# Row-sum reciprocals taken two tiles at a time, with each tile's probabilities made two steps behind its scores

## The chip, the cores and the metric

The kernel runs on one NeuronCore of a Trainium2 chip. The metric is the device time of one launch in microseconds (us); the core has a matrix engine (PE), a vector engine (DVE), a scalar engine (ACT), GpSimd (POOL), and a sync engine (SP) that issues the DMAs.

## The reference, cut to what matters

One decoder layer on x of shape 4 x 512 x 512 in float32: attention with low-rank query and key/value projections, 16 heads and rotary parts, then a quantised cross block, then a mixture of experts. The change touches the softmax of the attention:

```
scores = jnp.einsum('blhd,bmhd->bhlm', q, k) * scale
mask = jnp.tril(jnp.ones((L, L), bool))
scores = jnp.where(mask[None, None], scores, jnp.array(-1e+30, scores.dtype))
attn = jax.nn.softmax(scores, axis=-1)
out = jnp.einsum('bhlm,bmhd->blhd', attn, v)
```

With 4 batches and 16 heads there are 64 heads of 512 x 512 causal scores.

## The kernel before

Two heads make a pair, so `walk` runs over 32 pairs i = 0 to 31 (written out, no loop on the chip). A pair has eight steps g = 0 to 7: the four row tiles k = g & 3 of its first head, then those of its second. Tile k has (k + 1) x 128 columns, because of the causal mask. G = 8 i + g counts tiles over all pairs. Every engine has its own `pair` function with its instructions in a fixed order, and semaphores join the engines.

One tile goes through this chain:

- PE, `scores` (L1733 to L1738): six products into one of three PSUM banks.
- DVE, `row_max` (L1414): the negated row maximum. POOL, `bias` (L1018): times the scale.
- ACT, `exps` (L1160): the exponential into PF, with its row sum into one column of SUM.
- DVE, `row_scale` (L1421, L1423): reciprocal of the sum, times 4096.
- DVE, `probs_hi` (L1431) and `probs_lo` (L1438): the normalised tile as two fp16 parts in PH, high and rest.
- SP, `turn_probs` (L971): a DMA that transposes both parts into PT.
- PE, `values` (L1750): once for each head, after all its four transposes: the product with the values. `values(i, 0)` stands at step 7 of pair i, `values(i-1, 1)` at step 4.

Between these, each step carries other work. On DVE these are the low halves of two PSUM read-outs (`out_lo` L1444 at steps 0 and 5, `qn_lo_` L1449 at steps 2 and 6), the rotary part of the next pair (`rotate`, L1457, L1461 and L1462, at step 4; its copies L1466 and L1470 at step 7), and `add_y` (L1477). The rotary chain goes from `rotate` on DVE to `rope_sum` on POOL (L1022), `rope_hi` on ACT (L1176, L1177) and `rope_t_hi` on PE (L1690, step 6). On ACT, `out_hi` (L1165) of step 5 stands behind `rope_hi` in program order, and DVE's `out_lo` of step 5 waits for it. After `values(i, 0)` PE goes on with the scores of the next pair. From pair 4 on PE also runs `project` (L1765).

Even pairs below 24 also prepare a token tile of the next batch (`prep`): DVE's `prep_lo` (L1355, step 1) releases PE's `prep_t` (L1638), and later PE runs `prep_mm` (L1649). Pairs 24 to 31 have no such work.

At the end, SP issues `first_weights` (L369, four loads, 3 MB together) behind the transpose of tile 3 of pair 31 and ahead of those of tiles 4 to 7, on the same queue.

`turn_probs` and the release of `exps` wait on `s_lo`, the count of finished `probs_lo`; `probs_hi` waits until the tile before it in the same part of PH has been transposed.

Of the kernel before, what the change touches and what calls it, by code (L numbers as in the profile page):

```python
# [26 lines left out]
NPAIR = B * H // 2  # L27
# [3 lines left out]
PSCALE = 4096.0  # L31
# [4 lines left out]
def decoder_layer(nc, x, fside, ctxw, w_qa, q_norm_w, w_qb, w_kva, kv_norm_w, w_kvb, w_o,  # L36
                  router_w, w1, w2, w3, rope_tab, out):
    fp32, fp16, bf16, u32 = mybir.dt.float32, mybir.dt.float16, mybir.dt.bfloat16, mybir.dt.uint32
    ALU, ACT, AX = mybir.AluOpType, mybir.ActivationFunctionType, mybir.AxisListType
# [4 lines left out]
    def sem(name):  # L44
        return es.enter_context(nc.semaphore(name))
# [7 lines left out]
    with es:  # L53
# [26 lines left out]
        def take(cols, dt=fp32):  # L80
# [46 lines left out]
        NEGM, NB, SUM, RC, R4 = (small[:, 20 + 4 * k:24 + 4 * k] for k in range(5))  # L127
# [43 lines left out]
        s_mm, s_max, s_bias, s_exp, s_rc, s_hi, s_lo = (  # L171
            sem(n) for n in ("s_mm", "s_max", "s_bias", "s_exp", "s_rc", "s_hi", "s_lo"))
        pt_in = [sem(f"pt_in{k}") for k in range(TB)]
        s_r4 = sem("s_r4")
# [70 lines left out]
        def pf(k):  # L245
            return PF[:, k * (k + 1) // 2 * P:(k + 1) * (k + 2) // 2 * P]
# [4 lines left out]
        def ph_part(k, hl):  # L251

            return ph(k).rearrange("p (t l c) -> p t l c", l=2, c=P)[:, :, hl, :]
# [19 lines left out]
        def started(q):  # L273

            return not (isinstance(q, int) and q < 0)
# [960 lines left out]
        def _(dve):  # L1236
# [173 lines left out]
            def row_max(G, g):  # L1410

                n = ((g & 3) + 1) * P
                dve.wait_ge(s_mm, G + 1)
                dve.tensor_reduce(NEGM[:, (g & 3):(g & 3) + 1], banks[S_BANKS[g % 3]][:, 0:n], AX.X, ALU.max,  # L1414
                                  negate=True).then_inc(s_max, 1)

            def row_scale(G, g):

                k = g & 3
                dve.wait_ge(s_exp, G + 1)  # L1420
                dve.reciprocal(RC[:, k:k + 1], SUM[:, k:k + 1]).then_inc(s_rc, 1)  # L1421
                dve.wait_ge(s_rc, G + 1)
                dve.tensor_scalar(R4[:, k:k + 1], RC[:, k:k + 1], PSCALE, None, ALU.mult).then_inc(s_r4, 1)  # L1423

            def probs_hi(i, g):

                k, G = g & 3, 8 * i + g
                dve.wait_ge(s_r4, G + 1)
                if not (isinstance(i, int) and i == 0 and g < 4):
                    dve.wait_ge(pt_in[k], 16 * (2 * i + (g >> 2)))  # L1430
                dve.tensor_scalar(ph_part(k, 0), pf(k).rearrange("p (t c) -> p t c", c=P), R4[:, k:k + 1], None,  # L1431
                                  ALU.mult).then_inc(s_hi, 1)

            def probs_lo(G, g):

                k = g & 3
                dve.wait_ge(s_hi, G + 1)
                dve.scalar_tensor_tensor(out=ph_part(k, 1), in0=pf(k).rearrange("p (t c) -> p t c", c=P),  # L1438
                                         scalar=R4[:, k:k + 1], in1=ph_part(k, 0), op0=ALU.mult,
                                         op1=ALU.subtract).then_inc(s_lo, 1)  # L1440

            def out_lo(Hd, gpar, slot):
                dve.wait_ge(o_hi, Hd + 1)
                dve.tensor_tensor(ot(gpar, 1, slot, 0, L), banks[O_BANK][:, :], ot(gpar, 0, slot, 0, L),  # L1444
                                  ALU.subtract).then_inc(o_lo, 1)

            def qn_lo_(Hd, h):
                dve.wait_ge(qn_hi, Hd + 1)
                dve.tensor_tensor(qn(h, 1, 0, L), banks[Q_BANK][:, :], qn(h, 0, 0, L), ALU.subtract).then_inc(qn_lo, 1)  # L1449
# [14 lines left out]
            def rope_out_hi(i, par):  # L1464
                dve.wait_ge(r_th, i + 1)
                dve.tensor_copy(QR[:, par * 1536:par * 1536 + 1024], bank16[R_BANK]).then_inc(r_teh, 1)  # L1466

            def rope_out_lo(i, par):
                dve.wait_ge(r_tl, i + 1)
                dve.tensor_copy(QR[:, par * 1536 + 1024:(par + 1) * 1536],  # L1470
                                bank16[Q_BANK][:, 0:L]).then_inc(r_tel, 1)
# [8 lines left out]
            def pair(i, j, first=False, last=False, prep=None):  # L1480
                G = 8 * i
                for g in range(8):
                    if g == 7 and not last:
                        rope_out_hi(i + 1, 1 - j)
                    row_max(G + g, g)
                    if g > 0:
                        row_scale(G + g - 1, g - 1)
                    elif not first:
                        row_scale(G - 1, 7)

                    if g == 2:
                        qn_lo_(2 * i + 1, 1)
                    if g == 4 and not last:
                        rotate(i + 1)
                    if g == 5 and not first:
                        Hd = 2 * i - 1
                        out_lo(Hd, (Hd >> 3) & 1, Hd & 7)
                    if g == 6 and not last:
                        qn_lo_(2 * i + 2, 0)
                    if g == 7 and not last:  # L1500
                        rope_out_lo(i + 1, 1 - j)
                    if prep is not None and j == 0:
                        if g == 0:
                            prep_ln(prep[0])
                        if g == 1:
                            prep_lo(prep[0])
                    if g > 0:
                        probs_hi(i, g - 1)
                        probs_lo(G + g - 1, g - 1)
                    elif not first:  # L1510
                        probs_hi(i - 1, 7)
                        probs_lo(G - 1, 7)
                    if prep is not None and j == 0:
                        if g == 0:
                            prep_xn(prep[0])
                        if g == 3:
                            prep_var(prep[0])
                            prep_rope(prep[0], prep[2])
                            prep_srq(prep[0])
                            prep_rope_sum(prep[0])  # L1520
                        if g == 5:
                            prep_split(prep[0])
                    if g == 0 and not first:
                        Hd = 2 * i - 2
                        out_lo(Hd, (Hd >> 3) & 1, Hd & 7)
                    if prep is not None and j == 1 and g == 1:
                        prep_out(*prep)
                    if (j, g) in ADD and started(i - ADD[j, g]):
                        add_y(i - ADD[j, g])
# [39 lines left out]
            rope_out_lo(0, 0)  # L1569
            qn_lo_(0, 0)  # L1570
            walk(pair)
            row_scale(8 * NPAIR - 1, 7)
            probs_hi(NPAIR - 1, 7)
            probs_lo(8 * NPAIR - 1, 7)
            out_lo(2 * NPAIR - 2, 1, GH - 2)
            out_lo(2 * NPAIR - 1, 1, GH - 1)
            for q in range(NPAIR - 5, NPAIR):
# [290 lines left out]
```

## Time and profile before

| | |
|---|---|
| median of three runs | 1356.03 us (1355.33 to 1356.2) |
| profiled execution, device time | 1356.68 us |
| its span, first to last instruction | 1354.9 us |
| DVE busy | 1088.9 us (80%) |
| PE busy | 1039.2 us (77%) |
| ACT busy | 539.4 us (40%) |
| POOL busy | 239.7 us (18%) |
| pairs 0 to 31 | about 172 to 943 us of the span |

Times in a timeline count from the start of the span. A row of a timeline gives start, duration, engine, line, operation, output and input, and in brackets how long the engine had been idle and who ended that. DVE's durations overlap a little: the next instruction usually starts some 0.07 us before the last one's end is recorded. So what an instruction costs is read from start to start.

### The profile page before, as it was taken

The page shows a single profiled execution, that of the slowest core. Times are in us where ns is not written, and L with a number is a line of the kernel's source. Part 1 is how long each engine was busy: PE and PEld are TensorE (multiplying, and loading weights), DVE is VectorE, ACT ScalarE, POOL GpSimd, SP SyncE. Part 2 cuts the span into 40 slices and gives each one's busy share as a digit, 9 for nine tenths or more (in the row PEclk, how much of TensorE's full clock was granted, in tenths as well). Part 3 has the DMA queues.
Part 4 walks back from the last instruction along what each step waited for, and adds up shares of the span by engine and source line. Part 5 has one row for each costly group of instructions (what it writes and reads, how often), then busy time and mean ns, then how long its engine had stood idle before and what let it go on. Part 6 is the DMA issues. An engine that isn't in the chain of part 4 may idle for free.

```text
span 1354.9 us, 22533 instructions
## 1 busy us (share of the span) xinstructions
PE 1039.2 (77%) x7438; PEld 632.5 (47%) x7460; DVE 1088.9 (80%) x2984; ACT 539.4 (40%) x1225; POOL 239.7 (18%) x475
## 2 busy tenths in 40 slices
PE   1635687799999999998999999997743552547998
PEld 0423354455555555555555565564332231324554
DVE  5679587988888988988988988887179878876886
ACT  1539444434434434344444444443024321533443
POOL 1000012112112112112112121211022313131111
PEclk9659889999999999999999999999875776767999
DMA  9100022332332342322442333455361000000001
GB/s 360 55 1 0 1 53 49 73 58 57 58 56 54 65 116 53 66 55 46 70 119 47 66 61 61 94 92 147 79 218 39 24 31 0 0 0 8 39 31 47
DMA packets 199388, 86.30 MB, mean 64 GB/s; under 512 B 173560, under 2 KB 184824, under 8 KB 198784
## 3 DMA queue, kind: packets, MB, share of 16 engines
q1 hardware_dynamic: 199296, 85.12, 26.9%
q8 instruction: 52, 0.85, 0.3%
q14 instruction: 40, 0.33, 0.1%
HBM read 35.80 MB, written 7.34 MB: 32 GB/s over the span
## 4 chain that ended last, share of the span: by engine, by line
PE 40%; DVE 25%; issue 23%; ACT 5%; POOL 5%; DMA 1%; ACTq 0%; SPq 0%; DVEq 0%; POOLq 0%
PE bank L1765 10%; PE bank L1715 5%; DVE arena L1438 4%; PE bank L1649 4%; PE bank L1750 4%; DVE arena L1414 3%; PE bank L1681 2%; DVE arena L1431 2%; POOL arena L418 2%; PE bank L1733 2%; PE bank L1737 2%; PE bank L1735 2%; PE bank L1734 2%; PE bank L1736 2%; DVE scal L1532 1%
## 5 line engine op out<-in xcount | busy, mean ns | idle before, releaser
L1160 ACT ACTIVATE arena<-bank,arena,scal 128x128 f32<-128x128 f32 (+3 forms) x256 | 157.9, 617 | 356.6 <-POOL arena L1018 356.6
L1765 PE MATMUL bank<-arena 128*128 128x512 f16 x768 | 187.8, 391 | 7.1 <-DVE arena L1477 4.3
L1438 DVE SCALAR_TENSOR_TENSOR arena<-arena 128x128 f16<-128x128 f32 (+3 forms) x256 | 169.3, 661 | 9.1
L1414 DVE TENSOR_REDUCE arena<-bank 128x1 f32<-128x128 f32 (+3 forms) x256 | 124.2, 485 | 60.4 <-PE bank L1738 60.3
L1018 POOL TENSOR_TENSOR arena<-arena,scal 128x1 f32<-128x1 f32 x256 | 49.0, 191 | 551.2 <-DVE arena L1414 551.2
L1715 PE MATMUL bank<-arena 128*128 128x512 f16 x576 | 136.4, 382 | 0.5 <-DVE arena L1470 0.5
L1750 PE MATMUL bank<-arena 128*128 128x512 f16 (+3 forms) x768 | 116.8, 302 | 10.8 <-DMA arena<-arena 10.8
L1765 PEld LDWEIGHTS bank<-arena 128*128 128x128 f16 x768 | 73.6, 100 | 90.4 <-issue 16.5
L1431 DVE TENSOR_SCALAR arena<-arena 128x128 f16<-128x128 f32 (+3 forms) x256 | 109.9, 429 | 3.0 <-issue 0.3
L1750 PEld LDWEIGHTS bank<-arena 128*128 128x128 f16 x768 | 70.3, 99 | 50.4 <-issue 13.1
L1733 PE MATMUL bank<-arena 128*128 128x128 f16 (+3 forms) x256 | 77.3, 302 | 4.7 <-issue 3.3
L1715 PEld LDWEIGHTS bank<-arena 128*128 128x128 f16 x576 | 54.0, 99 | 55.5 <-issue 1.9
L1737 PE MATMUL bank<-arena 128*128 128x128 f16 (+3 forms) x256 | 77.3, 302 | 0.0
L1735 PE MATMUL bank<-arena 128*128 128x128 f16 (+3 forms) x256 | 77.3, 302 | 0.0
L1736 PE MATMUL bank<-arena 128*128 128x128 f16 (+3 forms) x256 | 77.3, 302 | 0.0
L1734 PE MATMUL bank<-arena 128*128 128x128 f16 (+3 forms) x256 | 77.3, 302 | 0.0
L816 PE MATMUL bank<-identb,arena 128*128 128x128 bf16 x192 | 24.7, 289 | 66.6 <-DVE arena L659 61.4
L1649 PE MATMUL bank<-arena 128*128 128x384 f16 (+1 forms) x384 | 59.0, 317 | 18.8 <-DVE arena L1259 15.3
L1681 PE MATMUL bank<-arena 128*128 128x128 f16 x1152 | 71.0, 221 | 1.5 <-DVE arena L1309 1.5
L1681 PEld LDWEIGHTS bank<-arena 128*128 128x128 f16 x1152 | 67.0, 99 | 5.8 <-DVE arena L1309 1.9
L1444 DVE TENSOR_TENSOR arena<-bank,arena 128x512 f16<-128x512 f32 x64 | 44.0, 688 | 28.8 <-ACT arena L1165 28.8
L1022 POOL TENSOR_TENSOR arena<-arena 128x512 f32<-128x512 f32 x32 | 45.8, 1430 | 109.7 <-DVE arena L1462 109.7
(213 smaller groups left out, 2119.7 us busy)
## 6 DMA issues: line engine op xcount, KB each, us to landing
arena<-in_L_attn_w_qb SPq DMA_DIRECT2D x1, 4608.0 KB, 23.5
arena<-in_x SPq DMA_DIRECT2D x4, 1024.0 KB, 5.9
arena<-in_L_attn_w_o SPq DMA_DIRECT2D x1, 4096.0 KB, 33.9
arena<-arena SPq DMA_TRANSPOSE x256, 2.8
arena<-in_fside_BxS2xS SPq DMA_DIRECT2D x4, 1024.0 KB, 5.7
arena<-in_L_ffn_w SPq DMA_DIRECT2D x8, 512.0 KB, 8.3
out<-arena SPq DMA_DIRECT2D x16, 256.0 KB, 2.0
arena<-in_x SPq DMA_DIRECT2D x12, 256.0 KB, 3.0
```

The costliest lines, as they stand in the source:

```text
L1160: act.activation(pf(k), banks[S_BANKS[g % 3]][:, 0:n], ACT.Exp, bias=NB[:, k:k + 1], scale=sc_exp, accum_out=SUM[:, k:k + 1]).then_inc(s_e ...
L1414: dve.tensor_reduce(NEGM[:, (g & 3):(g & 3) + 1], banks[S_BANKS[g % 3]][:, 0:n], AX.X, ALU.max, negate=True).then_inc(s_max, 1)
L1431: dve.tensor_scalar(ph_part(k, 0), pf(k).rearrange("p (t c) -> p t c", c=P), R4[:, k:k + 1], None, ALU.mult).then_inc(s_hi, 1)
L1438: dve.scalar_tensor_tensor(out=ph_part(k, 1), in0=pf(k).rearrange("p (t c) -> p t c", c=P), scalar=R4[:, k:k + 1], in1=ph_part(k, 0), op0= ...
L1649: last = pe.matmul(banks[bank][:, 0:wid], XNT[:, (a * DC + c) * P:(a * DC + c + 1) * P], WA[:, w:w + wid], start=(k == 0), stop=(k == 3 * ...
L1681: last = pe.matmul(banks[R_BANK][:, t * P:(t + 1) * P], ct(bp, a, c, t * P, P), wr(b, c, i & 7), start=(k == 0), stop=(k == 3 * QC - 1))
L1715: last = pe.matmul(banks[Q_BANK][:, :], wq(a, c, (i & 7) * 2 + h), ct(bp, b, c, 0, L), start=(k == 0), stop=(k == 3 * QC - 1))
L1733: pe.matmul(bank[:, 0:n], qn(h, 0, q, P), ct(bp, 0, QC, 0, n), start=True, stop=False)
L1734: pe.matmul(bank[:, 0:n], qn(h, 0, q, P), ct(bp, 1, QC, 0, n), start=False, stop=False)
L1735: pe.matmul(bank[:, 0:n], qn(h, 1, q, P), ct(bp, 0, QC, 0, n), start=False, stop=False)
L1750: last = pe.matmul(banks[O_BANK][:, kt * P:L], cn(bp, a, kt), pt(h, b, kt, kt * P, L - kt * P), start=(kt == 0 and n == 0), stop=(kt == TB ...
L1765: last = pe.matmul(banks[Y_BANK][:, :], ot(gp, a, k, (q & 3) * P, P), wo(b, gp * GH + k), start=(k == 0 and n == 0), stop=(k == GH - 1 and ...
```

## The change

`row_scale` becomes `row_scales`: on even steps only, one reciprocal and one multiplication of two adjacent columns, for the tiles of the two steps before. `probs_hi` and `probs_lo` of a tile move from one step behind its scores to two. After the last pair, two tiles instead of one are left to normalise.

```diff
-            def row_scale(G, g):
-                k = g & 3
-                dve.wait_ge(s_exp, G + 1)
-                dve.reciprocal(RC[:, k:k + 1], SUM[:, k:k + 1]).then_inc(s_rc, 1)
-                dve.wait_ge(s_rc, G + 1)
-                dve.tensor_scalar(R4[:, k:k + 1], RC[:, k:k + 1], PSCALE, None, ALU.mult).then_inc(s_r4, 1)
+            def row_scales(G):
+                k, n = G & 3, G // 2
+                dve.wait_ge(s_exp, G + 2)
+                dve.reciprocal(RC[:, k:k + 2], SUM[:, k:k + 2]).then_inc(s_rc, 1)
+                dve.wait_ge(s_rc, n + 1)
+                dve.tensor_scalar(R4[:, k:k + 2], RC[:, k:k + 2], PSCALE, None, ALU.mult).then_inc(s_r4, 1)
-            def probs_hi(i, g):
-                k, G = g & 3, 8 * i + g
-                dve.wait_ge(s_r4, G + 1)
-                if not (isinstance(i, int) and i == 0 and g < 4):
-                    dve.wait_ge(pt_in[k], 16 * (2 * i + (g >> 2)))
+            def probs_hi(G):
+                k = G & 3
+                dve.wait_ge(s_r4, G // 2 + 1)
+                if G >= 4:
+                    dve.wait_ge(pt_in[k], 16 * (G // 4))
@@ pair
                     row_max(G + g, g)
-                    if g > 0:
-                        row_scale(G + g - 1, g - 1)
-                    elif not first:
-                        row_scale(G - 1, 7)
+                    if g % 2 == 0 and G + g >= 2:
+                        row_scales(G + g - 2)
...
-                    if g > 0:
-                        probs_hi(i, g - 1)
-                        probs_lo(G + g - 1, g - 1)
-                    elif not first:
-                        probs_hi(i - 1, 7)
-                        probs_lo(G - 1, 7)
+                    if G + g >= 2:
+                        probs_hi(G + g - 2)
+                        probs_lo(G + g - 2, g - 2)
@@ after the walk
-            row_scale(8 * NPAIR - 1, 7)
-            probs_hi(NPAIR - 1, 7)
-            probs_lo(8 * NPAIR - 1, 7)
+            row_scales(8 * NPAIR - 2)
+            for g in (6, 7):
+                probs_hi(8 * NPAIR - 8 + g)
+                probs_lo(8 * NPAIR - 8 + g, g)
```

## Rows read from the trace of the kernel before

**Rows 1.** The page, part 2: busy tenths in 40 equal slices.

```profile
PE   1635687799999999998999999997743552547998
DVE  5679587988888988988988988887179878876886
```

**Rows 2.** Waits between 172 and 945 us: total us, times, longest.

```profile
DVE arena L1414 <- PE bank L1738: 59.7, 77, 2.4
...
PE bank L1690 <- ACT arena L1177: 32.4, 18, 3.9
PE bank L1638 <- DVE arena L1355: 13.1, 11, 2.8
```

**Rows 3.** DVE's groups of instructions: busy us, mean ns, idle before.

```profile
L1421 DVE RECIPROCAL arena<-arena 128x1 f32<-128x1 f32 x256 | 39.1, 153 | 0.0
...
L642 DVE RECIPROCAL arena<-arena 128x4 f32<-128x4 f32 x16 | 2.8, 178 | 0.6
```

**Rows 4.** Timeline of DVE in pair 17 (odd), and one `probs_lo` of 512 columns.

```profile
606.43 0.34 DVE L1431 TENSOR_SCALAR arena<-arena 128x256 f16<-128x256 f32 x1
...
606.81 0.48 DVE L1438 SCALAR_TENSOR_TENSOR arena<-arena 128x256 f16<-128x256 f32 x1
...
607.53 0.69 DVE L1414 TENSOR_REDUCE arena<-bank 128x1 f32<-128x512 f32 x1 [0.24 <-PE bank L1738]
608.13 0.15 DVE L1421 RECIPROCAL arena<-arena 128x1 f32<-128x1 f32 x1
...
608.51 0.61 DVE L1431 TENSOR_SCALAR arena<-arena 128x384 f16<-128x384 f32 x1
...
610.82 0.69 DVE L1457 TENSOR_TENSOR arena<-bank,arena 128x512 f32<-128x512 f32 x1
...
615.39 0.69 DVE L1444 TENSOR_TENSOR arena<-bank,arena 128x512 f16<-128x512 f32 x1 [0.56 <-ACT arena L1165]
...
624.48 0.75 DVE L1438 SCALAR_TENSOR_TENSOR arena<-arena 128x512 f16<-128x512 f32 x1
```

**Rows 5.** Timeline of PE in pair 17: last score product of tile 4, and `values(17, 0)`.

```profile
609.62 0.22 PE L1738 MATMUL bank<-maskb,identb 128*128 128x128 bf16 x1
...
619.76 1.79 PE L1750 MATMUL bank<-arena 128*128 128x512 f16 x12
```

**Rows 6.** SP's transpose of a 512-column tile of pair 17, issue and landing.

```profile
L971 SPq DMA_TRANSPOSE arena<-arena x1: 1232/1232/1232, 614.3 to 614.3; - x1
...
DMA to landing us min/median/max: 3.1/3.1/3.1
```

**Rows 7.** Timeline of DVE and of PE in pair 18 (even, with `prep`).

```profile
622.10 0.28 DVE L1414 TENSOR_REDUCE arena<-bank 128x1 f32<-128x128 f32 x1
...
639.12 0.69 DVE L1457 TENSOR_TENSOR arena<-bank,arena 128x512 f32<-128x512 f32 x1
...
643.23 0.62 PE L1690 MATMUL bank<-ident,arena 128*128 128x128 f16 x8 [2.25 <-ACT arena L1177]
...
650.12 0.22 PE L1733 MATMUL bank<-arena 128*128 128x128 f16 x1 [0.54 <-issue]
```

**Rows 8.** Timeline of PE in pair 16: `project` behind such a wait.

```profile
592.66 3.76 PE L1765 MATMUL bank<-arena 128*128 128x512 f16 x12 [0.18 <-DVE arena L1444]
```

**Rows 9.** Pair 26 (even, no `prep`): rotation on DVE, `values(26, 0)` on PE.

```profile
827.96 0.69 DVE L1457 TENSOR_TENSOR arena<-bank,arena 128x512 f32<-128x512 f32 x1
...
836.47 0.38 PE L1750 MATMUL bank<-arena 128*128 128x512 f16 x1
```

**Rows 10.** Pair 1 (no `project` yet): rotation on DVE, next pair's first scores on PE.

```profile
203.33 0.69 DVE L1457 TENSOR_TENSOR arena<-bank,arena 128x512 f32<-128x512 f32 x1
...
213.28 0.22 PE L1733 MATMUL bank<-arena 128*128 128x128 f16 x1 [0.55 <-issue]
```

**Rows 11.** After tile 3 of pair 31: SP's first loads, and PE's last `values`.

```profile
937.13 1.16 SPq L369 DMA_DIRECT2D arena<-in_fside_BxS2xS  x2
...
952.08 3.36 PE L1750 MATMUL bank<-arena 128*128 128x512 f16 x12 [10.84 <-DMA arena<-arena]
```

## The prediction

> **What bounds the kernel now.** I read the page's busy slices first. From slice 6 to slice 27, which are the 32 pairs, PE shows nines and DVE eights [rows 1]: two engines near full, so the question is which one waits for the other. The table of waits answers it. DVE's `row_max` waits 59.7 us in 77 waits for PE's scores, while PE waits 32.4 us for the rotary chain (L1690) and 13.1 us for `prep_lo` (L1638) [rows 2]. So PE sets the pace over long stretches, and DVE sets it at two places: before `prep_t` in even pairs, and, through POOL and ACT, before `rope_t_hi`. Work taken off DVE pays at those two places only. Then I read the timelines of one odd and one even pair and of an early and a late one, and asked for each new order when PE's next input would be there.
>
> **What is removed.** Each `row_scale` is two small operations; the reciprocal takes 153 ns, x256 [rows 3]. From the start of the reciprocal to the next operation the two take 608.51 - 608.13 = 0.38 us [rows 4]. Half of the 256 go: 128 x 0.38 = 48.6 us of DVE work. A two-column reciprocal is not in this kernel; it lies between one column (153 ns) and four columns (178 ns) [rows 3], and I take the first, since that difference is at most 0.03 us. If DVE were the bound throughout, 48 us would be gained. It is not.
>
> **What the saving moves.** In odd steps nothing stands between `row_max` and the step's other work, and DVE no longer waits there for ACT. Take pair 17. `row_max` of tile 3 is released by PE at 607.53 and the next operation starts 0.60 later. Before, `row_scale` and the tile of 384 columns followed. Now it is tile 1, 256 columns: 0.38 for L1431 and 0.41 for L1438 (0.48 less the overlap) [rows 4], so `add_y` (0.66) could begin at 608.92 and tile 4's `row_max` at 609.58. But PE ends those scores only at 609.62 + 0.22 = 609.84 [rows 5], so `row_max` starts at 609.87. The rotation follows 0.46 later, at 610.33 instead of 610.82: **0.49 us earlier**. In even pairs without `prep` DVE is further behind, and I take 0.68 (between 0.49 and 1.07, the sum of the 0.38, the smaller tile's 0.49 and 0.20; the wait for ACT's exponential takes the rest). In even pairs with `prep` the rotation does not move: DVE waits there for ACT's sums of squares, which hang on PE.
>
> At `prep_t` DVE runs unbroken from `row_max` of tile 0 (622.10 [rows 7]) to L1355. One `row_scale` on that stretch goes: 0.38 us earlier, out of a wait of 13.1 / 11 = 1.2 us [rows 2], so all of it counts, less any delay of that `row_max`.
>
> **What the move delays.** `values(i, 0)` at step 7 waits for the transposes of tiles 0 to 3. Tile 3, the largest, was normalised in step 4, right behind the rotation, and landed at 614.3 + 3.1 = 617.4 [rows 6], 2.4 us before PE came to it at 619.76 [rows 5]. Now it is normalised in step 5, behind `out_lo` (L1444), and `out_lo` waits for ACT's `out_hi`, which stands behind `rope_hi`, which waits for the rotation. So the time of landing hangs on the start R of the rotation:
>
> - R to `out_lo`: 615.39 - 610.82 = 4.57 [rows 4]
> - `out_lo` 0.61, `probs_hi` of 512 columns 0.52, `probs_lo` 0.75 [rows 4]: 6.45
> - to SP's issue 0.04, to landing 3.1 [rows 6]: 9.59
> - from landing to PE's start: not shown for this wait except at the very end, where some 0.25 lies between them. Bounds 0 and 0.4; I take 0.25: **R + 9.85**, with bounds R + 9.6 and R + 10.0.
>
> Tile 7's `values(i-1, 1)` at step 4 keeps 1.4 us or more of slack, by the same sum.
>
> The Trainium skill, page "DMA: Bandwidth & Descriptors", section "Anatomy of one DMA — SWDGE (gpsimd) path", gives a transfer about 2.0 us fixed and the rest by bytes over 436 GB/s. For this tile's 256 KB that would be an estimate of 2.6 us, R + 9.1 with nothing added, against the 3.1 us that the row shows; the section is written for another issuing path. By it the odd pairs would not wait at all, and the result would have the other sign (the first rival below).
>
> **Where PE then waits.** The next pair's scores can follow `values` 1.64 us after its start (3,840 columns at 2.4 GHz are 1.60).
>
> - Odd pairs 5 to 23 (10): PE comes at 619.76, which is 9.43 after the new R. Wait 0.42. In nine of them an even pair with `prep` follows: its tile 0 `row_max` starts 0.24 later than before (PE had 0.18 in hand), L1355 is 0.38 quicker, net -0.14: 9 x -0.14 = -1.3. Pair 23 has nothing behind it: +0.4.
> - Even pairs 4 to 22 (10): in six, PE runs at half clock after its 2.25 us wait [rows 7]: twelve L1765 products take 3.76 us [rows 8], where 12 x 512 columns at 2.4 GHz are 2.56. It then comes to `values` after R + 10, and the new wait is hidden. In four it does not slow, and the next scores start at R + 9.85 + 1.64 = R + 11.49 instead of 650.12 - 639.12 = 11.00 [rows 7]: 4 x 0.48 = +1.9. Their 0.54 us wait for L1470 hides the rest.
> - Pairs 24 to 30, where PE has no slack: pairs 26 and 30 start `values` at R + 8.51 [rows 9], now -0.68 + 9.85 - 8.51 = +0.66 each; pairs 24 and 28 already wait in `project` until about R + 9.28, so -0.11 each; pairs 25 and 27 +0.42 each, pair 29 about +0.7. Sum +2.6.
> - Pairs 0 to 3: PE is idle much of the time, DVE sets the pace. Odd ones reach the next scores at 213.28 - 203.33 = R + 9.95 [rows 10], now R + 11.49; DVE loses 1.18 of that, and gains 0.76 before the rotation and 0.38 before `prep_t`. Over all four I get +0.3.
> - The end: SP issues `first_weights` at 937.13, behind tile 3 of pair 31 [rows 11]. Tile 3 comes a step later, by my count at 937.1 instead of 935.86, so the 3 MB and the four transposes behind them shift by +1.2, and PE, which already waits 10.84 us for the last one [rows 11], with them.
>
> Sum: -1.3 + 0.4 + 1.9 + 2.6 + 0.3 + 1.2 = **+5.1 us**. Against the profiled execution (1356.68, its span plus 1.8) that is 1361.8. The median is 0.65 lower, so I say 1361.0.
>
> **Bounds.** The sum hangs on R + 9.85, which counts at some twenty places, about 2 us for each 0.1. At R + 9.6 it is -1 us, at R + 10.0 about +8.
>
> **The rivals.**
>
> *The transposes land in time, and the saving is left* (faster). If landing came by R + 9.1, odd pairs would not wait; the nine `prep_t` waits would give 0.56 each (5.0), the early pairs 2.2, the late ones 1.5, against 0.6 in four even pairs and about 0.7 at the end: -7.4, some 1349. It decides from R + 9.4 down. For it: PE has waits to give back [rows 2]. Against it: 3.1 us of landing in nearly every 512-column tile [rows 6].
>
> *It cancels* (no change): landing near R + 9.6 because PE starts at once when the transfer lands, or DVE runs further ahead than I allow. 1355 to 1358.
>
> *PE's clock* (slower still). After waits of 2.25 us PE fell to 1.2 GHz in six of ten pairs, at 1.0 us or more each [rows 7, 8]. If the new waits of 0.4 to 1.3 us brought that in a third of 25 places at 1.6 us, it would be +13 on top: 1374. Against it: the shortest wait behind which I find half clock is those 2.25 us, and behind four of the ten it did not come.
>
> *DVE is the bound after all*, and much of the 48 us comes: 1330 or less. DVE's own 59.7 us of waits for PE [rows 2] speak against it; I count it into the first rival.
>
> **How the numbers follow.** My forecast 0.56, in time 0.12, cancelled 0.24, clock 0.08. A change within 0.2% (2.7 us) is about what this kernel's measurement cannot tell from none. Slower takes the forecast but for its low end, and the clock: 0.61. Same 0.25, faster 0.14. The range leaves out the clock and most of the gain, takes both bounds of the sum and 2 us on either side: 1353.5 to 1367.
>
> **What the profile after would show.** L1421 and L1423 x128 at about 155 ns. A wait of PE's L1750 for the transposes in nearly all odd pairs, 0.3 to 0.5 us, and in late even pairs, over 0.7. Landing 9.6 after L1457's start. The wait at L1638 smaller by some 0.2 us a time, at L1690 unchanged at 2.25 in even pairs with `prep`, gone in the late ones. `first_weights` issued a microsecond later in its pair. DVE busy about 40 us less and its waits for PE up by about as much. The forecast is wrong if L1750 does not wait, if L1444 moves against the rotation, or if L1765 behind a short wait shows half clock.

## The result, and the profile after

The changed kernel takes **1373.49 us** (median of 4 runs, 1371.37 to 1373.84). The kernel before, on the same chip, takes 1355.68 us (4 runs). The medians differ by 17.8 us. The recorded ratio is 1.0117, with a 95% interval from 1.0091 to 1.0143, which is 16 us, with bounds of 12 and 19. I had said 1361.0, with a range up to 1367. The direction was right, the size was not: the loss is more than three times the one that I worked out, and lies outside the range.

The profiled execution took 1373.84 us, with a span of 1372.1. The page, part 2, of the changed kernel, beside [rows 1]:

```profile
PE   1625587799999998999999999989652643547998
DVE  5679576877877877877877888878169788886886
```

Many of DVE's eights became sevens: its busy time fell from 1088.9 to 1053.3 us. PE is as full as before, over a longer time. The groups of DVE say how much of the work went; beside [rows 3], reciprocals are half as many and hardly dearer:

```profile
L1423 DVE TENSOR_SCALAR arena<-arena 128x2 f32<-128x2 f32 x128 | 23.6, 184 | 4.4
...
L1421 DVE RECIPROCAL arena<-arena 128x2 f32<-128x2 f32 x128 | 19.8, 155 | 1.3 <-ACT arena L1160 1.0
```

The waits of the changed kernel from 172 to 960 us, beside [rows 2] (PE's lines are 4 lower now: L1634 is `prep_t`, L1686 `rope_t_hi`, L1698 `rope_t_lo`, L1746 `values`, L1761 `project`; DVE's have kept theirs):

```profile
DVE arena L1414 <- PE bank L1734: 87.5, 106, 3.2
...
PE bank L1686 <- ACT arena L1177: 30.8, 16, 3.8
...
PE bank L1746 <- DMA arena<-arena: 13.2, 13, 1.6
...
PE bank L1698 <- issue: 9.0, 6, 3.1
DVE arena L1477 <- DMA arena<-in_x: 8.1, 3, 3.4
...
PE bank L1634 <- DVE arena L1355: 6.2, 11, 1.5
```

The saving is there: the wait at `prep_t` fell from 13.1 to 6.2 us. What DVE no longer does it mostly waits for: 27.8 us more for PE's scores. Two waits are new. PE waits for transposed tiles before `values`, 13.2 us in 13 places. That kind of wait was forecast, but not these places: three are in pairs 1 to 3 (1.60, 0.60 and 1.63 us), and those of 1.18, 1.22 and 1.20 us in pairs 13, 21 and 29 come right behind the waits described next. And `add_y` (L1477) waits 8.1 us in three places for a load from `x`. Before, the same row was

```profile
DVE arena L1477 <- DMA arena<-in_x: 0.2, 1, 0.2
```

and my prediction does not mention it.

**Where the time went.** The rotation of each pair (L1457, start R) is a good milestone. Its start in the changed kernel less its start before, read from both timelines of DVE, in us:

| pair | 0 | 5 | 12 | 13 | 20 | 21 | 28 | 29 | 30 |
|---|---|---|---|---|---|---|---|---|---|
| later by | 0.1 | 5.8 | 7.0 | 8.5 | 9.1 | 11.4 | 12.9 | 15.8 | 16.3 |

So the 17.2 us between the spans fall into three parts: pairs 0 to 4 lose 5.8; three single steps, 12 to 13, 20 to 21 and 28 to 29, lose 1.46, 2.25 and 2.91, together 6.6; everything else, with 0.9 behind pair 30, makes 4.8.

**The forecast chain.** DVE and PE of pair 17, beside [rows 4] and [rows 5]; in brackets the idle time before:

```profile
618.82 0.29 DVE L1414 TENSOR_REDUCE arena<-bank 128x1 f32<-128x128 f32 x1 [0.21 <-PE bank L1734]
...
619.31 0.68 DVE L1457 TENSOR_TENSOR arena<-bank,arena 128x512 f32<-128x512 f32 x1
...
623.70 0.69 DVE L1444 TENSOR_TENSOR arena<-bank,arena 128x512 f16<-128x512 f32 x1 [0.95 <-ACT arena L1165]
624.30 0.48 DVE L1431 TENSOR_SCALAR arena<-arena 128x512 f16<-128x512 f32 x1
624.82 0.75 DVE L1438 SCALAR_TENSOR_TENSOR arena<-arena 128x512 f16<-128x512 f32 x1
```

and PE behind it:

```profile
628.99 1.79 PE L1746 MATMUL bank<-arena 128*128 128x512 f16 x12
```

`values` starts at 628.99 - 619.31 = R + 9.68. In the other pairs that wait for tile 3 it is R + 9.67 to 9.75, and 9.87 in pair 30. The forecast was 9.85; the difference is mostly that `out_lo` comes at R + 4.39 instead of 4.57.

**The early pairs.** PE in pair 1; the first row is the end of the rotary chain, the last the first scores of pair 2. R is 204.04.

```profile
211.75 0.38 PE L1698 MATMUL bank<-ident,arena 128*128 128x128 f16 x4 [2.02 <-issue]
213.73 3.36 PE L1746 MATMUL bank<-arena 128*128 128x512 f16 x12 [1.60 <-DMA arena<-arena]
216.88 0.31 PE L1729 MATMUL bank<-arena 128*128 128x128 f16 x1
```

The reader is to see two things. The wait of 1.60 us is the late tile, at R + 9.69. And the twelve products take 3.36 us instead of 1.79, so that the next scores come at R + 12.84, not R + 11.3. The granted clock says why (columns: stretch, length, PE busy with its instructions, clock, DMA share, GB/s):

```profile
211.70:212.50 0.80, 0.38 (x4) 1.00 1.11 212
212.50:213.70 1.20, 0.00 (x0) 0.53 0.47 92
213.70:216.90 3.20, 3.17 (x13) 0.50 0.23 46
```

PE stood idle for 2.02 us, worked for 0.38, stood idle for 1.60, and its clock fell to 0.50, the 1.2 GHz level. Before, PE waited 1.40 us at that place (L1702) and ran on at full clock. The two waits do not decide it alone: in run e1 below, whose code is the same here, pair 1 repeats this within 0.01 us, but in pair 3, behind waits of 2.02 and 1.59 us, the products ran at full clock:

```profile
264.10 0.38 PE L1698 MATMUL bank<-ident,arena 128*128 128x128 f16 x4 [2.02 <-issue]
...
266.08 1.79 PE L1746 MATMUL bank<-arena 128*128 128x512 f16 x12 [1.59 <-DMA arena<-arena]
```

**The single steps.** SP and DVE around pair 21 after the change; L929 is the load of the next batch's residual rows, 1 MB, which `reload_xa` issues behind the transpose of tile 7 of pairs 12, 20 and 28:

```profile
715.85 1.23 SPq L971 DMA_TRANSPOSE arena<-arena  x1
717.13 0.58 SPq L929 DMA_DIRECT2D arena<-in_x  x1
```
```profile
723.40 0.75 DVE L1477 SCALAR_TENSOR_TENSOR arena<-bank,scal,arena 128x512 f32<-128x512 f32 x1 [2.47 <-DMA arena<-in_x]
...
724.55 0.68 DVE L1457 TENSOR_TENSOR arena<-bank,arena 128x512 f32<-128x512 f32 x1
```

and the same three of the kernel before:

```profile
705.46 0.58 SPq L929 DMA_DIRECT2D arena<-in_x  x1
```
```profile
712.04 0.75 DVE L1477 SCALAR_TENSOR_TENSOR arena<-bank,scal,arena 128x512 f32<-128x512 f32 x1
...
713.17 0.69 DVE L1457 TENSOR_TENSOR arena<-bank,arena 128x512 f32<-128x512 f32 x1
```

The kernel as a whole is 9.1 us late in pair 20, but the load is issued 11.7 us late, since tile 7 comes a step later and SP, which issues in program order, issues the load behind it. It lands 6.2 us after its issue, at 723.3, and `add_y`, which stands just ahead of the rotation, waits 2.47 us for it. Before, it landed at 711.1 and `add_y` began 0.9 later: that was all the cover there was. At pair 13 the cover was 0.5 us, and at pair 29 none: there `add_y` already waited 0.20.

### The profile page after: what moved, and what is told of

Read it like the earlier page. It is cut to its first block, busy times and chain, and to the rows that moved or that the text cites. A ratio compares the mean times of both kernels' runs of the same rounds, so it can differ in the third digit from the quotient of the medians.

```text
span 1372.1 us, 22299 instructions
## 1 busy us (share of the span) xinstructions
PE 1049.2 (76%) x7460; PEld 634.6 (46%) x7460; DVE 1053.3 (77%) x2728; ACT 539.2 (39%) x1225; POOL 241.0 (18%) x475
## 4 chain that ended last, share of the span: by engine, by line
PE 36%; issue 26%; DVE 20%; POOL 7%; ACT 5%; DMA 5%; SPq 0%; ACTq 0%; DVEq 0%; POOLq 0%
PE bank L1761 8%; PE bank L1746 6%; PE bank L1645 4%; PE bank L1711 4%; DMA arena<-arena 3%; POOL arena L1022 2%; DVE arena L1414 2%; POOL arena L418 2%; PE bank L1677 2%; DVE arena L1431 2%; DVE arena L1438 2%; PE bank L1729 1%; PE bank L1731 1%; PE bank L1733 1%; PE bank L1730 1%
## 5 line engine op out<-in xcount | busy, mean ns | idle before, releaser
L1761 PE MATMUL bank<-arena 128*128 128x512 f16 x768 | 193.4, 400 | 7.4 <-DVE arena L1477 3.7
L1438 DVE SCALAR_TENSOR_TENSOR arena<-arena 128x128 f16<-128x128 f32 (+3 forms) x256 | 159.3, 622 | 9.1
L1018 POOL TENSOR_TENSOR arena<-arena,scal 128x1 f32<-128x1 f32 x256 | 57.5, 225 | 561.1 <-DVE arena L1414 561.1
L1746 PE MATMUL bank<-arena 128*128 128x512 f16 (+3 forms) x768 | 121.3, 310 | 25.0 <-DMA arena<-arena 23.5
L1711 PE MATMUL bank<-arena 128*128 128x512 f16 x576 | 137.2, 384 | 0.5 <-DVE arena L1470 0.5
L1761 PEld LDWEIGHTS bank<-arena 128*128 128x128 f16 x768 | 74.8, 102 | 93.6 <-issue 21.8
L1746 PEld LDWEIGHTS bank<-arena 128*128 128x128 f16 x768 | 71.3, 101 | 70.4 <-issue 34.2
L1711 PEld LDWEIGHTS bank<-arena 128*128 128x128 f16 x576 | 54.3, 99 | 56.0 <-issue 2.9
L1677 PEld LDWEIGHTS bank<-arena 128*128 128x128 f16 x1152 | 67.3, 99 | 5.6 <-DVE arena L1309 1.9
L885 PE MATMUL bank<-arena 128*128 128x512 bf16 x256 | 60.0, 389 | 0.2 <-issue 0.2
```

The lines of the kernel that those rows point to most:

```text
L1677: last = pe.matmul(banks[R_BANK][:, t * P:(t + 1) * P], ct(bp, a, c, t * P, P), wr(b, c, i & 7), start=(k == 0), stop=(k == 3 * QC - 1))
L1711: last = pe.matmul(banks[Q_BANK][:, :], wq(a, c, (i & 7) * 2 + h), ct(bp, b, c, 0, L), start=(k == 0), stop=(k == 3 * QC - 1))
L1746: last = pe.matmul(banks[O_BANK][:, kt * P:L], cn(bp, a, kt), pt(h, b, kt, kt * P, L - kt * P), start=(kt == 0 and n == 0), stop=(kt == TB ...
L1761: last = pe.matmul(banks[Y_BANK][:, :], ot(gp, a, k, (q & 3) * P, P), wo(b, gp * GH + k), start=(k == 0 and n == 0), stop=(k == GH - 1 and ...
```

## The experiments

Shifts of R are against the profile of the kernel before, as in the table above. In the kernels with a plan, `scale_to(s)` and `probs_to(t)` take the reciprocals and the normalised tiles up to a tile, two reciprocals in one operation where two are due, and `return s, t, u` gives both limits for the usual places of a step and `u` for `probs_to` behind the step's `out_lo`; T is 8 i + g. The kernel after is `(T - 1 if g % 2 == 0 else T - 2), T - 2, T - 2`; the kernel before is `T - 1, T - 1, T - 1`.

**e9, only SP's store and load moved.** The kernel before, with the 1 MB store of the residual rows and their reload a step later, and nothing else:

```diff
-                    if i % 8 == 4 and i >= 12:
-                        if g == 3:
-                            store_xa(i // 8 - 1)
-                        if g == 7:
-                            reload_xa(i // 8)
+                    if i % 8 == 4 and i >= 12 and g == 4:
+                        store_xa(i // 8 - 1)
+                    if i % 8 == 5 and i >= 13 and g == 0:
+                        reload_xa(i // 8)
```

> The kernel before, with two of SP's instructions alone one step later: the store of XA behind the transpose of tile 4 instead of tile 3, and the 1 MB reload of XA behind the transpose of tile 0 of the next pair instead of behind that of tile 7. That is where the change puts them in time; everything else is as before. If the jumps of 1.5, 2.3 and 2.9 us seen after the change at pairs 13, 21 and 29 come from the later reload, this kernel shows add_y (L1477) waiting for the load in those three pairs, some 1 to 3 us each, and ends 3 to 6 us above the kernel before: 1359 to 1362. If those jumps came from the later tiles themselves, it is within 1.5 us of the kernel before and L1477 waits for nothing.

Measured: 1359.24 us (12 runs) against 1355.98 (17), ratio 1.0036 [1.0020, 1.0051]. The waits:

```profile
DVE arena L1476 <- DMA arena<-in_x: 3.4, 3, 1.5
```

R jumps at exactly the three pairs, by 0.80, 1.00 and 1.29. The mechanism is shown: two DMA issues moved by one step make 3.1 us of jumps, and 3.3 us in the medians. That is half of the 6.6 of the changed kernel, where the waits were 2.24, 2.47 and 3.41 instead of 1.00, 0.94 and 1.50: there the load is later still (against R by 1.6, 2.5 and 2.4 us, here by 1.4, 1.8 and 1.8), and DVE comes to `add_y` sooner.

**e5 and e6, a quarter of the reload.** Both kernels with the load cut to 256 KB:

```diff
                 sp.wait_ge(xa_out, 16 * b)
-                load_xa(b)
+                sp.dma_start(XA[:, 0:D], x[b][0:P, :]).then_inc(xa_in, 16)
```

> The kernel before with the reload of XA in pairs 12, 20 and 28 cut from 1 MB to its first 256 KB (three quarters of the next batch's residual rows are left out, so the output is not the reference's). It is the base for the next run. Theory (before, the reload lands in time and does not hold PE): within 2 us of before.

> The changed kernel with the same cut reload. Theory (about 6.6 us of the 17 are the reload, 1 MB long, slipping by a step with tile 7 on the sync engine's queue, and add_y waiting for it): L1477's 8.1 us of waits for in_x fall to under 1 us, the rotation of pair 30 comes 5 to 6.5 us earlier than in the changed kernel, and the distance to the run beside it is 10 to 12 us. Rival (jumps at pairs 13, 21 and 29 have another cause): the rotation of pair 30 stays within 2 us of the changed kernel's.

Measured: e5 1355.37 us (10 runs), ratio 0.9992 [0.9978, 1.0007]; e6 1366.28 us (5 runs), ratio 1.0069 [1.0046, 1.0093]. The kernel before loses nothing by the load, the changed one some 7 us. In e6 the jumps of R are -0.8, -0.6 and +0.8 instead of 1.46, 2.25 and 2.91, and one wait of `add_y` is left:

```profile
DVE arena L1477 <- DMA arena<-in_x: 1.3, 1, 1.3
```

The distance to e5, 10.9 us, is as expected. But R30 is 10.9 us earlier than in the changed kernel, where I expected 5 to 6.5, and 2.6 of that comes in pairs 0 to 5, which the edit does not touch: from pair 0 to pair 5 e6 loses 3.2 us, the changed kernel 5.8. PE's clock fell at other places. In pair 1 the twelve products took 1.79 us behind a wait of 1.62, in pair 3 they took 3.36. So what the early pairs lose differs from one execution to another, by as much as some of the terms below.

**e1, the reload ahead of tile 7's transpose.** The kernel after, with

```diff
+                    if i % 8 == 4 and i >= 12 and g == 7:
+                        reload_xa(i // 8)
                     turn_probs(i, g)
...
-                        if g == 7:
-                            reload_xa(i // 8)
```

> The changed kernel with one thing moved on the sync engine's queue: the reload of XA in pairs 12, 20 and 28 is issued ahead of the transpose of tile 7, not behind it. Theory (the reload slipped by a step with tile 7, and add_y three steps later waits for it): L1477 no longer waits 8.1 us for in_x, rotation of pairs 13, 21 and 29 comes 1.3 to 2.8 us earlier, 5 to 6.5 us in all, so about 1367.5 us. Rival (the jumps at these pairs are the value products' own waits or the clock): 1372 us or more.

Measured: 1376.13 us (4 runs, 1366.69 to 1377.34), ratio 1.0112 [1.0061, 1.0163], not to be told from the changed kernel. My expectation missed. The waits of `add_y` halved, but others grew:

```profile
PE bank L1746 <- DMA arena<-arena: 16.6, 14, 3.1
...
DVE arena L1477 <- DMA arena<-in_x: 3.9, 3, 2.1
```

Tile 7's transpose now stands behind 1 MB: the transposes issued behind the load took up to 8.2 us to land, and PE waits for them 0.95, 2.62 and 3.08 us in pairs 13, 21 and 29. Behind the two longer waits its twelve products took 3.18 and 3.36 us instead of 1.79. The late tile and the load share a queue, and with tile 7 two steps behind either order loses.

**e10, tile 3 alone a step later.** By the plan, all else as before:

```diff
+                if g == 4:
+                    return T - 1, T - 2, T - 2
+                return T - 1, T - 1, T - 1
```

> The kernel before, with tile 3 of each head pair's first head alone normalised a step later, behind out_lo of step 5 and just ahead of tile 4; all other tiles one step behind their scores, one reciprocal for each tile, the reload behind tile 7 as before. So it has the late landing without the saving and without the later reload. By the landing theory values starts at R + 9.7 (R is the rotation, L1457) and PE waits for the transfer in pairs 1 to 3 by about 1.6 us, with half clock behind it, and by 0.2 to 1.2 us in later pairs; no wait of L1477 beyond the kernel before's 0.2. I expect 5 us by pair 5 and 4 to 8 more by pair 30: 1364 to 1369. If instead the pairing of reciprocals or the delay of the other seven tiles made the early loss, pairs 0 to 4 keep their time within 1.5 us and the whole is under 1361.

Measured: **1385.91 us** (5 runs), ratio 1.0212 [1.0196, 1.0227], the slowest of all. The waits of `out_lo` for `out_hi`, of PE for the transposes and of `add_y` for the load (L1448 is `out_lo` here, L1770 `values`, L1481 `add_y`):

```profile
DVE arena L1448 <- ACT arena L1165: 73.3, 30, 2.5
...
PE bank L1770 <- DMA arena<-arena: 17.2, 19, 2.1
...
DVE arena L1481 <- DMA arena<-in_x: 0.3, 1, 0.3
```

`values` starts at R + 9.71 to 9.88 in most waiting pairs. R is 9.3 us late by pair 5 and 26.9 by pair 30, some 0.7 a pair; in the odd pairs `values` starts at R + 9.8 instead of 8.94, and the next scores at R + 11.4 instead of 10.57, so nearly all of the lateness is passed on. I expected a loss of 8 to 13 us and measured 29.9. Moving tile 3 alone loses more than the whole change does, but not by the change's path alone. This kernel leaves step 4 without a tile and puts two, 3 and 4, into step 5. DVE, with no more than a `row_max` and a `row_scale` to do between the rotation and `out_lo`, stands idle there, 2.42 us in pair 17:

```profile
630.45 0.69 DVE L1448 TENSOR_TENSOR arena<-bank,arena 128x512 f16<-128x512 f32 x1 [2.42 <-ACT arena L1165]
```

`out_lo` comes at R + 4.40, no sooner than with a tile ahead of it. These waits are 73.3 us in all, against the following before and 28.5 us after the change, where tile 2 stands in that place:

```profile
DVE arena L1444 <- ACT arena L1165: 16.8, 30, 0.6
```

So e10 shows the landing at R + 9.7 and PE's waits without the pairing and without the late load, but its 29.9 us are not the price of tile 3's lateness in the changed kernel.

**e2, the delay without the pairing.** The kernel after, but one reciprocal for each tile:

```diff
-                return (T - 1 if g % 2 == 0 else T - 2), T - 2, T - 2
+                return T - 1, T - 2, T - 2
```

> The delay alone: probabilities two steps behind the scores as in the changed kernel, but one reciprocal and one multiplication a tile in every step, as before. Theory (the delay costs, and the 48 us taken off DVE give back only some microseconds): 1374 to 1380 us, the value products waiting as in the changed kernel. Rival (pairing costs, because DVE waits for two exponentials): clearly below 1373, towards 1356.

Measured: 1380.80 us (4 runs), ratio 1.0164 [1.0127, 1.0201]; R30 is 21.3 late. So the pairing gives back some 5 to 7 us of the 48.6 that I worked out as DVE's saving: 7.3 by the medians, 5.1 by R30, of which 1.7 are longer waits for the load. e10 is slower than e2 although it delays one tile in eight and leaves the load alone. What e2 has besides is tile 2 between the rotation and `out_lo`, so that DVE waits there 20.8 us and not 73.3, and a smaller tile ahead of the rotation, which was not tried by itself.

**e3 and e7, the early pairs.** e3 keeps the old order in pairs 0 to 4. e7 is the kernel after with PE given something to do in pairs 0 to 3, `busy(16)` ahead of `rope_t_lo` and again ahead of `values`: sixteen transposes of the 128 x 128 identity into a bank that is free there. First e3's edit, then e7's:

```diff
+                if i < 5:
+                    return T - 1, T - 1, T - 1
                 return (T - 1 if g % 2 == 0 else T - 2), T - 2, T - 2
```
```diff
                         if g == 7:
+                            if i < 4:
+                                busy(16)
                             rope_t_lo(i + 1)
+                            if i < 4:
+                                busy(16)
```

> Pairs 0 to 4 in the order of before, all later pairs in that of the change. Theory (5.5 us are lost in the first pairs, where PE, waiting for the transposes, also falls to 1.2 GHz): rotation of pair 5 within 0.5 us of before, total about 1368 us. Rival (these pairs lose nothing that later waits would not take anyway): 1372 to 1374 us.

> The changed kernel with 16 idle transposes of the identity on PE ahead of rope_t_lo and 16 more ahead of the value products of step 7, in pairs 0 to 3 alone; they fill PE's waits there. Theory (of the 6.5 us lost by pair 5, about half are the waits themselves and half is PE at 1.2 GHz behind them): values and the next scores at 2.4 GHz in pairs 1 and 2 (about 1.6 us from value products to next scores, not 2.5 to 3.1), the rotation of pair 5 2 to 4 us earlier. Rival (half clock there costs nothing, DVE being the pace): the rotation of pair 5 within 0.5 us of the changed kernel's.

Measured: e3 1372.02 us (4 runs), ratio 1.0109 [1.0073, 1.0145]; e7 1369.35 us (4 runs), ratio 1.0087 [1.0062, 1.0112]. In e7, pair 1 of PE:

```profile
208.33 1.06 PE L1769 MATMUL bank<-ident 128*128 128x128 f16 x16
210.09 1.79 PE L1746 MATMUL bank<-arena 128*128 128x512 f16 x12 [0.70 <-DMA arena<-arena]
```

The tile comes no sooner, but the twelve products take 1.79 us, at full clock, and the next scores follow at R + 11.3 to 11.5 in pairs 1 to 3. From pair 0 to pair 5 R loses 3.1 us in e7 against 5.8, which is 2.7 us less, as I had expected. But e6 loses only 3.2 there without any such work, and in e7 the clock fell in pair 3 at another place, some 17 us behind R. So the 2.7 us are not shown to be the clock's price. The profiles, one for each kernel, give this loss from pair 0 to pair 5: with the order of the change 5.8 (after), 6.2 (e1) and 3.2 (e6), with the old order 0 (before), -0.5 (e3), 0.5 (e9), 2.9 (e8 and e11) and 3.4 (e5). In e5, e8 and e11 the clock stayed down in pair 2 until `values` was through (3.1 us instead of 1.79), and fell in pair 4, where before it did not. The new order is the slower one here, by some 3.5 us between the means of three profiles and of six; the 5.8 of one profile is not its price.

In e3 the early loss is gone (R5 is 0.7 early, R30 is 6.9 late instead of 16.3), yet the median is only 1.5 us lower, within the range that I had given for the rival: in its profile the stages behind pair 30 took 448.0 us, against 441.6 before and 442.5 after. These kernels differ there by up to 7 us (440.9 to 448.0) though their code there is the same. Part of it is PE's clock. About the same 20 us of that stage, first of e3, then of the kernel before:

```profile
1174.00:1194.00 20.00, 16.15 (x87) 0.72 0.00 0
```
```profile
1164.00:1184.00 20.00, 15.22 (x91) 0.90 0.00 0
```

What decides it was not found. So the positions of R tell the terms apart better than the medians do, and I lean on them, with the spread in the early pairs in mind.

**e4, tiles 3 and 7 in time, the others paired and late.**

```diff
+                if g % 4 == 0:
+                    return T - 1, T - 2, T - 1
                 return (T - 1 if g % 2 == 0 else T - 2), T - 2, T - 2
```

> Reciprocals paired as in the change, but tiles 3 and 7 normalised at the end of steps 4 and 0, right behind tiles 2 and 6, so one step behind their scores as before; steps 5 and 1 normalise nothing. Theory (the loss is tile 3 and tile 7 being late, for the value products and for what stands behind tile 7 on the sync engine's queue): no waits of the value products, and the saving shows: 1347 to 1355 us. Rival (DVE's changed order itself costs PE): 1360 us or more.

Measured: 1359.27 us (10 runs), ratio 1.0013 [0.9997, 1.0030], not to be told from the kernel before, and above the 1347 to 1355 that I expected. With the two tiles that a head's `values` waits for last back in their steps, 14 of the 17.8 us are gone. This is the plainest evidence that the lateness of these two, with what hangs on it, is most of the loss. From pair 0 to pair 5 this kernel still loses 3.5 us, though tile 3 is in time, with `values` of pair 2 at half clock (3.36 us). What keeps it from being faster is that step 0 now carries two tiles: `prep_t` (L1658) waits longer than in either kernel, and `add_y` still waits for the load.

```profile
PE bank L1658 <- DVE arena L1355: 20.7, 11, 3.5
...
DVE arena L1481 <- DMA arena<-in_x: 6.6, 3, 3.0
```

**e8, what is best of this.** The old order in pairs 0 to 4, tile 3 always in time, tile 7 in time except where `prep` follows:

```diff
+                if i < 5:
+                    return T - 1, T - 1, T - 1
+                if g == 4 or (g == 0 and (i % 2 == 1 or i >= 24)):
+                    return T - 1, T - 2, T - 1
                 return (T - 1 if g % 2 == 0 else T - 2), T - 2, T - 2
```

> Reciprocals paired from pair 5 on, pairs 0 to 4 in the order of before. Tile 3 always normalised at the end of step 4, behind tile 2. Tile 7 at the end of step 0 where the pair has no prep, otherwise in step 1 as in the change. Theory (the losses are tile 3 late, the early pairs and the reload; the saving on DVE is worth 0.3 to 0.6 us a pair where DVE paces): rotation of pair 30 2 to 6 us earlier than before, 1350 to 1355 us. Rival (the saving is worth nothing, because PE paces): 1355 to 1358 us.

Measured: 1359.59 us (10 runs), ratio 1.0025 [1.0012, 1.0039], above both ranges that I had given. From pair 5 to pair 28 R gains 1.4 us, and at pair 29 the load's wait costs 1.8. With the losses taken out, the saving is worth a microsecond or two; no version here beats the kernel before.

**e11, both causes out.** The kernel after with the edits of e3 and e6:

> The changed kernel with both named causes taken out at once: pairs 0 to 4 in the old order, and the reload of the residual rows cut to 256 KB (three quarters of the next batch's residual rows are left out). Compare with the kernel before under the same cut (1355.4), and with the changed kernel under it (1366.3). If the two causes are separate and add, this one is 1358 to 1361: what is left are some 3 to 5 us, the waits for tile 3 in the late pairs and the tail. If pair 0 to 4's loss returns elsewhere, or a third cause is missing, it is 1363 or more; if the saving were worth something once the losses are out, it is under 1355.

Measured: 1362.36 us (7 runs, 1359.17 to 1367.57), ratio 1.0049 [1.0030, 1.0068]. That is 1.4 us above what I expected for two causes that add, and 0.6 under what a third would need; runs that lie 8 us apart do not tell these two apart. Its R is 3.1 us late at pair 5 although the order there is the old one: PE reached the `values` of pair 4 at R + 10.96 instead of 9.28, its clock having fallen on the way. e8, with the old order too, shows the same 3.1, and e5, whose order is the old one all through, loses some 4 us in pairs 2 to 12 after an early start. So that much can happen to the old order as well. From pair 5 on R moves from 3.1 to 3.8 by pair 23, and to 5.9 by pair 30: +0.7 and +2.0.

## Why the prediction was wrong in size

**Right.** The engine that sets the pace: 48.6 us of DVE's work went (35.6 of its busy time), and 5 to 7 of the time came of it (e2 against after). The late landing: R + 9.70 for a forecast of R + 9.85. The sum for the pairs from 5 on, once the load is out of the way: pairs 4 to 22, forecast -1.3 + 1.9 = +0.6, measured +0.7 in e11 from pair 5 on; pairs 23 to 30, forecast 0.4 + 2.6, measured +2.0 (in e6 +0.2 and +2.4). In the changed kernel itself, pairs 26 and 30 wait as forecast, over 0.7 us:

```profile
849.67 1.79 PE L1746 MATMUL bank<-arena 128*128 128x512 f16 x12 [0.97 <-DMA arena<-arena]
```

There R is 839.96, so this is R + 9.71, beside R + 8.51 in [rows 9]. The end, too: `first_weights` is issued behind a later tile 3, and PE's last `values` starts 2.1 us later against R30 than before (forecast 1.2), of which 0.9 is left at the end.

```profile
956.12 1.16 SPq L369 DMA_DIRECT2D arena<-in_fside_BxS2xS  x2
```
```profile
970.45 3.36 PE L1746 MATMUL bank<-arena 128*128 128x512 f16 x12 [10.34 <-DMA arena<-arena]
```

**The rivals.** The transposes do not land in time: every pair that waits for tile 3 shows R + 9.7 to 9.9, and odd pairs would have had to see R + 9.4. So the first rival falls, and with it the estimate from the Trainium skill (page "DMA: Bandwidth & Descriptors", section "Anatomy of one DMA — SWDGE (gpsimd) path"). Its 2.6 us for the 256 KB do not agree with these transposes, which SP issues and which took 3.0 to 3.1. "It cancels" falls by the whole result, although e11's pairs 5 to 22 come near it. DVE is not the bound: its waits for PE grew. The clock rival holds in part, below. The new waits of 0.46 to 1.22 us from pair 13 on left `values` at full clock.

**Sizes slightly off, with no weight in the sum.** The odd pairs with `prep` behind them wait 0.15 to 0.2 us, not 0.3 to 0.5, since the chain is 0.15 shorter. `prep_t` waits 0.63 us less a time, not 0.2. The two-column multiplication takes 184 ns; only the reciprocal is as cheap as one column. And the low end of the bounds was summed wrongly: by 2 us for each 0.1, R + 9.6 makes +0.1, not -1.

**Wrong, first: what stands behind a moved transpose.** The step "What the move delays" followed the transposes of tiles 3 and 7 to the engine that waits for them, and stopped there, except at the end. It said of tile 7 that it "keeps 1.4 us or more of slack", which is true of the tile. But SP issues its DMAs in program order, and behind tile 7 of three pairs stands a load of 1 MB that had 0.5, 0.9 and no us to spare. The prediction has no term for it: 0 for 6.6 us measured. e9 shows the mechanism alone, at half the size, and e6 shows it all but gone. I had applied the very same reasoning to `first_weights` in pair 31, 3 MB behind tile 3, and had not asked which other loads the queue holds.

**Wrong, second: the term for pairs 0 to 3,** +0.3 where 5.8 were measured in the profile, and 3.2 in that of e6. It took the next scores to follow 1.64 us behind `values`, at full clock, and let DVE lose 1.18 an odd pair. They came 3.15, 2.99 and 2.09 behind it in pairs 1 to 3. This is the rival of PE's clock, at three places instead of a third of 25. Against that rival I had held that the shortest wait with half clock behind it was 2.25 us, and weighed only the new wait of up to 1.3. PE already waited at `rope_t_lo`, a few instructions ahead, and the new wait came on top: 2.02 and 1.60 us, with 0.38 of work between. I had also let DVE's gains ahead of the rotation count in pairs where PE's wait came behind it. How the 5.8 divide between the clock and the tile's lateness is not shown: e7 lost 2.7 less with PE kept busy, and e6 2.6 less without. e3 speaks for the order in these pairs as the cause; e2 and e10, which lose 6.9 and 9.9 us from pair 0 to pair 5 with the reciprocals unpaired, show that the pairing is not needed for it. Not all of it is tile 3: e4, with tile 3 in time, loses 3.5, and part is the luck of the execution, since the old order itself lost 3.4 in e5.

**The account.** Forecast +5.1. The load adds 6.6 and the early pairs 5.5 more: 17.2, which is the measured difference of the spans. That it fits to the tenth is chance, since the other terms are right only within a microsecond, since the early pairs vary by 3 us with the same code, and since the stages behind pair 30 vary from kernel to kernel by more than that. The bounds did not cover it because both ends of the sum came from one number, R + 9.85. An order of work that moves eight tiles in each of 32 pairs had more ways to lose than that one.

**Open.** Why the stages behind the last pair take 440.9 to 448.0 us with the same instructions; what decides whether PE's clock falls in the early pairs, and what each fall costs; and what tile 3 a step later costs by itself, with another tile left in its place, since e10 left that place empty.

## What to carry to other kernels

When an operation moves a step, follow its DMA in both directions of the queue: who waits for it, and what is issued behind it. Write down every load on that queue with its spare time (here 0 to 0.9 us for 1 MB), before any sum. Delay is charged to the last tile that a consumer needs, while a saving on an engine that does not set the pace comes back only in part, here 5 to 7 of 48 us; so count the consumer's deadline first. A new wait on PE is to be weighed with those that stand close before it: here 1.60 us came on top of 2.02, and the clock fell. And before a loss read from one profile is given a cause, look for the same code in the profiles of the other kernels: here 5.8 us were 3.2 elsewhere.

## What the runs showed of the hardware

- PE at 1.2 GHz behind idle times of 2.02 and 1.60 us with 0.38 us of work between them, the granted clock 0.50; with 1.06 us of dummy transposes ahead of each wait, the same twelve products ran at full clock (1.79 us instead of 3.36). The same idle times do not always bring it: in pair 3 of e1, behind 2.02 and 1.59 us with 0.38 between, the products took 1.79 us.
- The 1 MB load from DRAM landed 5.6 to 6.3 us after its issue in both kernels, and the transpose of a 512-column tile mostly 3.0 to 3.2 us after its own. Transposes issued right behind such a load took up to 8.2 us (e1), and PE waited up to 3.1 us for them. With the late transpose issued first, `add_y` waited up to 3.4 us for the load.
- The hand-over from the rotation on DVE to POOL and ACT became 0.19 us shorter (`rope_t_hi` at R + 3.92 instead of 4.11) with no instruction of that chain changed; only what DVE does next had changed. The cause was not looked for.
